# Layer 0 of a selective-scan kernel: six of sixteen sources scaled by ScalarE on the transposed side, sums over states as transposes

## The reference, cut to what matters

```python
def step(h, inp):
    ul, dl, bl, cl = inp
    dA = jnp.exp(dl[..., None] * A)
    h = dA * h + (dl * ul)[..., None] * bl[:, :, None, :]
    y = jnp.einsum('bkdn,bkn->bkd', h, cl)
    return (h, y)
```

## Time and profile before

| | |
|---|---|
| median of 3 runs | 15647.34 us |
| lowest, highest | 15642.23, 15655.48 us |
| span of the profiled execution | 15638.3 us |
| DVE busy | 14604.3 us (93%) |
| POOL busy | 13820.4 us (88%) |
| PE busy | 12948.2 us (83%) |
| ACT busy | 8897.0 us (57%) |
| mean granted TensorE clock | 0.946 of 2.4 GHz |

### The profile page before, as it was taken

One profiled execution on the slowest core, in us unless ns is written; L12 is line 12 of the kernel. 1 busy time (PEld: TensorE's weight loads), 2 busy tenths in 40 slices (PEclk: granted clock), 3 DMA queues, 4 the chain that ended last, 5 costly groups with the idle time before them and its releaser, 6 DMA issues.

```text
span 15638.3 us, 128313 instructions
## 1 busy us (share of the span) xinstructions
PE 12948.2 (83%) x42560; PEld 7615.4 (49%) x42560; DVE 14604.3 (93%) x8593; ACT 8897.0 (57%) x8571; POOL 13820.4 (88%) x5892
## 2 busy tenths in 40 slices
PE   7887888878888788887888878888788887888878
PEld 4553355533555335553355533555335553355533
DVE  8998989989899899998999989999899998999988
ACT  4455745457454674556744567445674456744567
POOL 7997979979799798997989978899788997889978
PEclk8999999999999999999999999999999999999999
DMA  5662256622566225662256622566225662256622
GB/s 180 211 214 104 86 180 213 211 101 86 185 212 211 100 84 187 214 210 98 82 193 212 210 95 81 193 213 213 93 78 199 213 211 92 76 200 213 211 87 77
DMA packets 696921, 2473.06 MB, mean 158 GB/s; under 512 B 79292, under 2 KB 101064, under 8 KB 696264
## 3 DMA queue, kind: packets, MB, share of 16 engines
q1 hardware_dynamic: 696264, 2464.85, 45.9%
HBM read 2448.81 MB, written 15.73 MB: 158 GB/s over the span
## 4 chain that ended last, share of the span: by engine, by line
POOL 47%; issue 18%; DVE 13%; PE 11%; DMA 7%; ACT 3%; DVEq 0%; POOLq 0%; SPq 0%; ACTq 0%
POOL room L1043 24%; POOL room L1086 7%; DMA room<-bc_rows 7%; POOL room L1052 5%; POOL room L1078 4%; POOL room L1089 4%; DVE room L1279 4%; DVE room L1212 3%; PE bank L621 3%; POOL room L1033 3%; DVE room L1220 3%; PE bank L556 2%; PE bank L407 2%; DVE u L1169 1%; DVE room L1299 1%
## 5 line engine op out<-in xcount | busy, mean ns | idle before, releaser
L1043 POOL TENSOR_TENSOR room<-room 128x1024 f32<-128x1024 f32 x3072 | 7161.8, 2369 | 0.6
L1212 DVE TENSOR_TENSOR_SCAN room<-bank,room 128x1024 f32<-128x1024 f32 x3072 | 6936.5, 2278 | 75.7 <-POOL room L1043 71.7
L556 PE MATMUL bank<-room,identity 128*128 128x256 f32 x24576 | 5985.2, 389 | 188.5 <-DVE room L1220 188.5
L556 PEld LDWEIGHTS bank<-room,identity 128*128 128x128 f32 x24576 | 4758.9, 195 | 1333.5 <-DVE room L1220 269.6
L825 ACT ACTIVATE bank<-room,a 128x1024 f32<-128x1024 f32 x3072 | 3411.3, 1115 | 3273.9 <-DVE room L1212 3258.4
L621 PE MATMUL bank<-room,identity 128*128 128x512 f32 x6144 | 3011.5, 641 | 860.8 <-DVE room L1299 728.4
L1279 DVE TENSOR_TENSOR_SCAN room<-bank,room 128x1024 f32<-128x1024 f32 x1536 | 3431.5, 2274 | 54.1 <-POOL room L1086 33.6
L1220 DVE TENSOR_TENSOR room<-room,bank 128x1024 f32<-128x1024 f32 x2304 | 2764.1, 1200 | 387.3 <-PE bank L526 374.1
L621 PEld LDWEIGHTS bank<-room,identity 128*128 128x128 f32 x6144 | 1204.8, 204 | 2667.3 <-issue 1257.2
L1086 POOL TENSOR_TENSOR room<-room 128x1024 f32<-128x1024 f32 x768 | 2224.3, 2919 | 56.2 <-ACT room L908 26.7
L1052 POOL TENSOR_TENSOR room<-room 128x1024 f32<-128x1024 f32 x768 | 1817.1, 2366 | 344.1 <-DVE room L1212 343.0
(11 more groups left out here) (115 smaller groups left out, 8767.1 us busy)
## 6 DMA issues: line engine op xcount, KB each, us to landing
room<-bc_rows SPq DMA_DIRECT2D x4608, 512.0 KB, 4.4
wx<-in_w_x SPq DMA_DIRECT2D x65, 162.0 KB
bc_rows<-xdbl SPq DMA_DIRECT2D x72, 128.0 KB, 5.3
pictures<-in_x SPq DMA_DIRECT2D x8, 768.0 KB, 10.9
out_x<-pictures SPq DMA_DIRECT2D x8, 768.0 KB, 7.2
win<-in_w_in SPq DMA_DIRECT2D x16, 288.0 KB, 6.1
room<-in_w_in SPq DMA_DIRECT2D x16, 288.0 KB, 5.0
room<-in_w_out SPq DMA_DIRECT2D x16, 288.0 KB, 5.6
```

The lines of the kernel that those rows point to most:

```text
L556: ins = nc.tensor.matmul(dst[line][part], identity[:, :], src[line][part], start=(i == 0 and n == 0 and line == 0), stop=(n == N - 1 and l ...
L1043: nc.gpsimd.tensor_tensor(source0[:, g % SOURCES, :], du0[:, j, :], b_ring0[:, g % BROWS, :], ALU.mult).then_inc(S["source"], note("source ...
L1212: nc.vector.tensor_tensor_scan(run(state0[:, g % STATES, :]), run(whole(DECAY0[g % 2])), run(source0[:, g % SOURCES, :]), 0.0, ALU.mult, A ...
```

## The change

Only layer 0 changes.

1. **Six sources a pass by another way.** `by_turn` names n in (1, 5, 7, 9, 12, 15) in every pass but the first of an image. For them PE turns du once a pass (`turn_du`, eight 128 x 128 transposes) and ACT keeps it (`keep_du`); B is turned once a direction (`turn_b`, `keep_b`). With pixels on partitions, B[n] is one number a partition: ACT makes the turned source in eight 128 x 128 pieces with a per-partition scale (`scale_source`, four of them three units ahead, four two units ahead), and PE turns it back into the PSUM buffer that would have held the decay (`turn_source`, eight transposes, after the scan two units back). ACT then writes the decay of such a unit into a source slot in SBUF, and the scan reads the two with places exchanged. The DMA of the B row falls away, and `b_ring0` has 3 slots.
2. **Sums over states on the turned side.** `sum_states` is eight transposes that add in PSUM, in place of four matmuls. ACT copies the sum (`y_turned`), PE turns it back into WORK at n = 9 of the next pass (`turn_back`), and DVE adds it to y after the scan of n = 10, in two strided halves (`collect`). PE no longer puts y back (L544 before).
3. **Weighing.** POOL weighs n in (2, 4, 5, 6, 8, 9, 11, 12), DVE the other eight.
4. The pieces move to other n, most to units that POOL weighs: xd to (0,4), (0,6), (0,8), (1,2); dt to n = 2 or, for j = 1, n = 6.

```diff
+def by_turn(i, j, n):
+    return i * J + j > 0 and n in (1, 5, 7, 9, 12, 15)
...
-    return n in (2, 5, 8, 11)
+    return n in (2, 4, 5, 6, 8, 9, 11, 12)
...
+    if n == 12 and ahead - 1 < PASSES:
+        return "du", ahead - 1
+    if n == 9 and i * J + j > 0:
+        return "y", i * J + j - 1
...
+            def turn_source(b, g):
+                s = TURNED.index(UNITS[g]) % 2
+                pe.wait_ge(S["scan"], at("scan", UNITS[g - 2], b))
+                pe.wait_ge(S["scaled"], at("scaled", UNITS[g], b))
+                for k in range(CHUNKS):
+                    ins = nc.tensor.matmul(whole(DECAY0[g % 2])[:, k * P:(k + 1) * P],
+                                           source_turned[:, s, k * P:(k + 1) * P], identity[:, :],
+                                           start=True, stop=True, is_transpose=True)
...
             def sum_states(b, g):
...
-                for h in range(2):
-                    for line in range(2):
-                        part = lines_in(SCANS[i][1], h, 2, line)
-                        ins = nc.tensor.matmul(dst[line][part], identity[:, :], src[line][part],
...
+                for k in range(CHUNKS):
+                    ins = nc.tensor.matmul(whole(YACC)[:, k * P:(k + 1) * P], state0[:, g % STATES, k * P:(k + 1) * P],
+                                           identity[:, :], start=(n == 0 and k % 4 == 0),
+                                           stop=(n == N - 1 and k % 4 == 3), is_transpose=True)
...
+            def scale_source(b, g, ks):
...
+                for k in ks:
+                    cut = slice(k * P, (k + 1) * P)
+                    ins = nc.scalar.activation(source_turned[:, t % 2, cut], du_turned[:, (i * J + j) % 2, cut],
+                                               ACT.Identity, scale=b_turned[:, i % 2, k, n:n + 1])
...
+                    for ahead, ks in ((3, range(CHUNKS // 2)), (2, range(CHUNKS // 2, CHUNKS))):
+                        if g + ahead < len(UNITS) and by_turn(*UNITS[g + ahead]):
+                            scale_source(b, g + ahead, ks)
```

More of the change, by code:

```diff
@@ L70, in piece @@
     ahead = i * J + j + 2
[L71 removed]
+    if n == (6 if j == 1 else 2) and ahead < PASSES:
         return "dt", ahead // J, ahead % J
+    if n == 12 and ahead - 1 < PASSES:
+        return "du", ahead - 1
+    if n == 9 and i * J + j > 0:
+        return "y", i * J + j - 1
+    if i < K - 1 and (j, n) == (1, 8):
+        return "b", i + 1
     if i < K - 1 and (j, n) in QUARTERS:
@@ L238, in program @@
                  "p1", "p2", "parts", "dl", "du",
-                 "decay", "source", "scan", "spread", "weigh", "weigh_pool", "sum",
+                 "decay", "source", "source_turned", "scan", "turn_du", "du_turned", "turn_b", "b_turned", "scaled", "spread", "weigh", "weigh_pool", "sum",
                  "dcol", "cs", "drows", "dcols", "gate", "source1", "gated", "gated_last", "ones", "scan1", "hsum", "weigh1", "sum1",
-                 "yinit", "yev", "ysum", "cen", "sq", "rs", "nrm", "aff", "gat", "res"]
+                 "yinit", "yev", "y_turned", "y_back", "ysum", "cen", "sq", "rs", "nrm", "aff", "gat", "res"]
         S = {n: semaphore("s_" + n) for n in names}
@@ L533, in begin_sums @@
                 if n == 0 and i * J + j > 0:
[L534 to L538, removed]
+                    pe.wait_ge(S["y_turned"], at("y_turned", i * J + j - 1, b))
                 if g == 0 and b > 0:
                     pe.wait_ge(S["ev"], at("ev", ("out", 1, 0), b - 1))
-                if n == 0 and i > 0:
-                    for h in range(2):
-                        nc.tensor.matmul(bank[:, YACC + h, :], identity[:, :], y[:, j, halves(h)],
-                                         start=True, stop=False)
             def sum_states(b, g):
@@ L1203, in scan @@
                 dve.wait_ge(S["decay"], at("decay", (i, j, n), b))
-                dve.wait_ge(S["source"], at("source", (i, j, n), b))
+                decays, sources = whole(DECAY0[g % 2]), source0[:, g % SOURCES, :]
+                if by_turn(i, j, n):
+                    dve.wait_ge(S["source_turned"], at("source_turned", (i, j, n), b))
+                    decays, sources = sources, decays
+                else:
+                    dve.wait_ge(S["source"], at("source", (i, j, n), b))
                 if g >= STATES:
@@ L1211, in scan @@
                     dve.wait_ge(S["res"], at("res", (1, 1), b - 1))
-                nc.vector.tensor_tensor_scan(run(state0[:, g % STATES, :]), run(whole(DECAY0[g % 2])),
-                                             run(source0[:, g % SOURCES, :]), 0.0, ALU.mult, ALU.add).then_inc(
-                    S["scan"], note("scan", (i, j, n)))
+                nc.vector.tensor_tensor_scan(run(state0[:, g % STATES, :]), run(decays), run(sources), 0.0,
+                                             ALU.mult, ALU.add).then_inc(S["scan"], note("scan", (i, j, n)))
             def weigh(b, g):
@@ L1232, in scans0 @@
                         i, j, n = UNITS[g]
+                    if g < len(UNITS) and n == 10 and i * J + j > 0:
+                        collect(b, i * J + j - 1)
                     if g > 0 and not by_pool(*UNITS[g - 1]):
```

154 lines of the change are left out of this document (118 added, 36 removed).

## The result

| | before | after |
|---|---|---|
| median us | 15650.53 (4 runs) | 16335.42 (4 runs) |
| span of the profiled execution | 15638.3 | 16333.6 |
| mean granted clock, of 2.4 GHz | 0.946 | 0.855 |

The ratio is 1.0441, interval 1.0426 to 1.0455: the change makes the kernel **4.4% slower**. 15,240 was forecast, and the range ended at 15,720. The forecast was wrong, and on the wrong side.

A forecast was written before the change was run, and what follows sets the result against it. DVE and POOL, both full, bound layer 0 at 50.4 us a pass. DVE's 45.3, scan 15's wait 2.6 and the remainders make 48.1: 51 us less an image, 408 in all, from 15638: 15240, range up to 15,720.

The forecast's parts named there:

- its loop: POOL and DVE in turn, from one weighing of state 2 to the next: 45.9 us a pass, hidden under the pass.
- The stall of scan 15: DVE waits for ACT, which does decay 14, copy, four pieces, softplus and decay 15 in 8.1 us: 2.6 a pass.
- the step on PE: PE's work a pass: 24 sets of eight transposes at 0.11 each, 21 us, plus 8.3 for the rest: 29.4 of 48.1.
- The stall of 1.9: Before the change, 1.9 us a pass, mostly spreads behind a piece on PE before DVE's weighings; claimed to go.
- the forecast's own signs of being wrong: Layer 0's clock near 0.5, turned scans waiting for PE, slower POOL operations or scans, or idle time before weighings again.
- the remainders ahead of it: In a third of the passes remainders sit on ACT just ahead of scan 15's wait: the pass goes from 47.9 to 48.1.
- 46.3 + 8.8: First pass of an image: POOL's work from scan 2 to the next pass's first source, 46.3; then three scans, two weighings, 8.8.
- R2: PE's clock falls but a transpose stays at 0.11; PE late, not the bound: 50.3 a pass, 15650, no change; chance 0.13.
- R1: PE's clock falls to 1.2 GHz, a transpose takes 0.211 and PE bounds: 57 a pass, 16,900; chance 0.13.
- R3: ACT is dearer, scaled pieces at 0.385, scan 15 waits 3.0: 49.5 a pass, 15,500; chance 0.12.
- R4: Scan 15 doesn't wait, the loop of POOL and DVE bounds: 46.2 a pass, 14,900; chance 0.06.
- R5: The change doesn't do what it says, sources and weighings stay where they were; excluded by POOL's order, no chance given.

The follow-up runs named there:

- the tenth experiment: The changed kernel with softplus moved from n = 14 to n = 0 of the next pass and 25 useless filling matmuls a pass on PE: 15248.03 us, 0.9745 of before.
- The probes: Two small kernels without the network that time transposes and ordinary products on PE: transposes alone 0.109 us apart; equal work of both kinds stood at equal clock levels.
- the paced probe: Own kernel without the network; PE and ACT take turns, 60 steps per kind and number of products: 8 transposes 1.97 us, 4 ordinary 2.07, 16 transposes 1.97, 8 ordinary 2.05.
- the first probe: Own kernel without the network; PE does 60 sets of eight transposes, then of ordinary products: 480 transposes in 55.3 us, 0.213 us apart for the first 5.6 us, then 0.109.

## Why the prediction was wrong

**Right.** A transpose at full clock is 0.109 after the one before (eight in 1.04 us); 0.11 was taken. "Four times faster" in the table of terms of the Trainium skill's "TensorE: Matmul & The Clock Gate" isn't borne out: an ordinary product of the same tile is two records 0.112 apart, so twice is what the runs show. A scan keeps its 2.20 with the operands exchanged (mean 2282 ns beside 2274). POOL's operations stay at 2.31 and its loop lies hidden. A scaled piece lasts 388 ns and follows the last by 0.29, where 0.275 was taken. The stall of scan 15 was forecast at 2.6 us a pass, and stands where it was forecast, 0.6 larger. DVE's groups from 2187 to 3417 us, layer 0 of the second image behind its first pass, give it as 73 us in 22.8 passes (365 scans by 16), 3.2 a pass:

```profile
L1320 DVE TENSOR_TENSOR_SCAN room<-bank,room 128x1024 f32<-128x1024 f32 x228 | 515.1, 2273 | 7.6 <-ACT bank L889 7.2 <-issue 0.4
L1320 DVE TENSOR_TENSOR_SCAN room<-room,bank 128x1024 f32<-128x1024 f32 x137 | 312.6, 2282 | 80.1 <-ACT room L889 73.1 <-PE bank L578 4.8 <-issue 2.0
L1327 DVE TENSOR_TENSOR room<-room,bank 128x1024 f32<-128x1024 f32 x182 | 218.7, 1202 | 45.8 <-PE bank L547 45.6
L1342 DVE TENSOR_TENSOR y<-y,bank 128x512 f32<-128x512 f32 x40 | 34.3, 902 | 37.1 <-PE bank L605 37.1
L1339 DVE SCALAR_TENSOR_TENSOR y<-u,skip,bank 128x512 f32<-128x512 f32 x6 | 4.2, 740 | 4.7 <-PE bank L605 4.7
```

**Wrong: the step on PE.** The forecast added 29.4 of 48.1 us and found the tightest place with 2.2 us for a set that needs 0.9. All of that was counted at 2.4 GHz, and DVE's waits for PE were put at nothing: "The stall of 1.9 should go". They are 4.1 us a pass. With the clock at 0.97 (the tenth experiment) the waits before weighings do go, but for the starts of the images, so the order of the pieces was sound and the clock was what the step had wrong. The low clock was seen and put into two rivals, with 0.13 each, mainly under the condition that transposes might not count. But PE had been busy 1008 of 1190 us while the clock stood at 0.97, and the forecast itself took it down to 61%, where no row showed which level it would have. At 80 to 100 us, with few matmuls, the clock stood at 0.51. The same sum that made PE look harmless was the warning. One of the forecast's own signs of being wrong, idle time before the weighings again, came true.

**What stands in its place.** By the same groups a pass takes 53.9 us (1230 in 22.8 passes). DVE's idle time is 175.3 us, 7.7 a pass; the other 46.2 are its work, start to start, where 45.3 was forecast.

| a pass, us | forecast | measured |
|---|---|---|
| DVE's work | 45.3 | 46.2 |
| waits for ACT (forecast 2.6, and 0.2 for the remainders ahead of it) | 2.8 | 3.5 |
| waits for PE (weighings 2.0, collect 1.8, turned scans 0.2) and issue (0.1) | 0 | 4.2 |
| sum | 48.1 | 53.9 |

Waits make 4.9 of the 5.8 us, PE alone 4.1. DVE's work is 0.9 more: the two halves of the collect last 0.90 each where 1.25 was taken for both, and an instruction that comes after a wait doesn't overlap the one before it. The difference of 5.8 over 8 x 23 passes is 1070 of the 1095 us by which the forecast missed. The first pass of an image takes the rest: POOL's second weighing of state 2 came 57.5 us after the first (2127.61 to 2185.10), where the forecast's terms give 46.3 + 8.8 = 55.1. PE's 4.1 are not the cost of the clock alone: the earlier y shows that places in the queue play a part. By the tenth experiment about three quarters of these waits go when the filling brings the clock back; queue and clock weren't separated further.

Three figures of the forecast don't follow from its rows, and carry nothing: the dear end of an ordinary fp32 matmul (0.22 + 0.19 is 0.41, not 0.43), the dear end of a scaled piece (0.225 + 0.07 + 0.1 is 0.395, not 0.385; 0.388 was measured), and "68% of PE's time would be busy", where its own sum gives 61%. Of the 374 us before weighings that it spread over the passes, 107 stood at the starts of images.

**The rivals.** R2 named the mechanism: PE at half speed isn't the bound but is late, at spreads and at xd and y. Its premise that a transpose stays at 0.11 fails (0.213 at the lower level). Its size was too small (50.3 a pass with the softplus), since it counted one late spread in two passes of three and 1.7 us behind xd, where the runs have 2.0 before weighings and 1.8 before collects; and its reason, that transposes might not count, isn't borne out. The Trainium skill, "TensorE: Matmul & The Clock Gate", Part 4, "PE-mode transpose", has it that transposes don't engage the upper level. The probes disagree: transposes alone reached 0.109 us each, and 16 in a step of 3.1 us kept the upper level as eight ordinary products did. R1's price for a transpose at the low clock was right (0.211 forecast, 0.213 measured), but PE wasn't the bound, because the low clock holds for part of the time only. R3, R4 and R5 didn't happen: pieces cost what was taken, scan 15 waits, and POOL's and DVE's work went as written.

**What would have made it right.** With the softplus moved and PE's pauses filled, the same change gives 15248 us, 8 from the forecast. That nearness is partly chance, since the stall of 2.6 us a pass that the forecast contains (478 us in all) is gone in that version and other waits (100.3 and 145.6 for ACT, 92.5 for POOL, 203 for PE) remain. What it does show is that the change has a gain of about the size forecast, 2.6%, once two waits of its own making are taken out.

## What to carry to other kernels

Work taken off PE isn't free of consequence: count how full PE is after the change, and if it is much emptier than in the stretch whose clock you know, price all of PE's places once more at half speed, with the queue behind each. Don't look for the cause of a low clock at the largest stall alone: with the softplus moved the stall was gone and the clock went from 0.82 to 0.83 only. Useless matmuls in PE's pauses can pay, here 466 us; and steps with a fixed cost such as a softplus between two table loads belong where the next step isn't due soon, here 564 us.

## What was unexpected of the hardware

- A PE that does less work can need more time for it: PE's busy time in layer 0 fell from 1008 to 859 of 1190 us, and DVE's waits for it grew.
- fp32 transposes of 128 x 128 follow one another at 0.109 us at 2.4 GHz and at 0.213 at 1.2 GHz; an ordinary product of the same tile takes two records 0.112 apart. Where the two kinds were given equal work, the clock stood at the same level.
- The clock fell even after pauses that are short. In the paced probe PE never stood still for more than 1.15 us, and four ordinary products a step let the clock fall from the upper level. Eight transposes a step stayed at half speed while 16, which fill the same 1.97 us at twice the speed, kept it up. So steps with PE busy 1.97 of 3.1 us were seen at either level.
- The clock also fell with PE almost full: before the change 14 of 15 falls of layer 0's first image stand right behind the projection with 12 rows, at 505.6 us with PE busy 8.89 of the 10 us before 505.
- In the paced probe the profile's clock column stood at 1.00 over the first stretch, where the eight transposes took 1.97 us, and so it did over the slow start of the first probe: there the durations tell the level and the column doesn't.
